# Destination scores split once in bfloat16 parts before the look-up, and 40 key scatters moved behind the first stream's gathers

## The reference

```python
# first graph attention
z  = einsum('ni,hid->nhd', xn, W)
es = einsum('nhd,hd->nh', z, a_src);  ed = einsum('nhd,hd->nh', z, a_dst)
e  = es[src] + ed[dst]
e  = where(e >= 0, e, 0.01 * e)
alpha = exp(e - segment_max(e, dst)[dst]) / segment_sum(..., dst)[dst]
out   = segment_sum(alpha[:, :, None] * z[src], dst)
x = x + out + linear_attention(xn)
# second graph attention, over the layernorm of the new x, 4 experts x 4 heads
e  = leaky_relu(a_src[src] + a_dst[dst], 0.2)     # edges of L0_ffn_edge_index and own edges
...                                                # aggregate, layernorm, top 2 of 4 experts
x = x + sum over experts of gate * (gelu(xn @ W1 + b1) @ W2 + b2)
```

## Time and profile before

| | us |
|---|---|
| median of three runs | 6389.44 |
| lowest and highest run | 6359.07, 6403.71 |
| profiled execution, span from first to last instruction | 6245.5 |
| first look-up stage in it, from POOL's first scatter to DVE's last reduction | 363.4 to 619.8 |
| second look-up stage, from POOL's first gather to DVE's last reduction | 3456.0 to 3632.4 |

### The profile page before, as it was taken

How to read it: one execution, slowest core, us unless ns; L and a number is a source line. 1 busy time by engine, 2 the same in 40 slices (tenths; PEclk the granted TensorE clock), 3 DMA queues, 4 the chain that set the end, 5 groups by cost and what they waited for, 6 DMA issues and landing times. The chain is left out here.

```text
span 6245.5 us, 58318 instructions
## 1 busy us (share of the span) xinstructions
PE 3399.7 (54%) x14771; PEld 2497.0 (40%) x14771; DVE 2946.1 (47%) x6874; ACT 1902.2 (30%) x6108; POOL 3158.9 (51%) x3144
## 2 busy tenths in 40 slices
PE   5554356565666666655552634555455554555660
...
GB/s 109 74 207 166 104 93 95 95 96 91 95 101 106 105 106 109 106 100 96 93 76 52 223 109 24 26 26 27 24 25 31 23 30 24 25 31 22 30 34 248
DMA packets 326836, 508.54 MB, mean 81 GB/s; under 512 B 102092, under 2 KB 249219, under 8 KB 314654
## 3 DMA queue, kind: packets, MB, share of 16 engines
...
...
## 5 line engine op out<-in xcount | busy, mean ns | idle before, releaser
L1440 POOL DMA_INDIRECT gnn_gathered<-gnn_rows,gnn_src x1612 | 1603.5, 995 | 970.2 <-issue 454.4
L1929 POOL DMA_INDIRECT ffn_gathered<-ffn_rows,ffn_src x1216 | 1201.9, 988 | 1249.8 <-DVE ffn_scaled L2335 807.9
L1528 PE MATMUL gnn_step_ps<-gnn_scaled,gnn_dst_onehot 128*128 128x260 f32 x3224 | 1209.8, 517 | 820.2 <-DVE gnn_scaled L1622 585.3
L1467 ACT ACTIVATE gnn_scaled<-gnn_gathered,gnn_edge_weights 128x65 f32<-128x65 f32 x4464 | 1137.4, 336 | 778.2 <-remote 377.5
L1528 PEld LDWEIGHTS gnn_step_ps<-gnn_scaled,gnn_dst_onehot 128*128 128x128 f32 x3224 | 746.7, 252 | 1122.6 <-DVE gnn_scaled L1622 674.2
L1642 DVE TENSOR_TENSOR gnn_sums<-gnn_sums,gnn_step_ps 128x260 f32 x1612 | 680.5, 422 | 623.9 <-PE gnn_step_ps L1528 252.0
L2054 PE MATMUL exp_hidden_ps<-exp_xn_turned,exp_w 128*128 128x512 f32 (+1 forms) x832 | 532.5, 777 | 486.4 <-ACT exp_hidden L2085 342.5
L2238 PE MATMUL ffn_sum_ps<-ffn_scaled,ffn_dst_onehot 128*128 128x24 f32 x2432 | 392.6, 320 | 350.6 <-issue 234.3
L2085 ACT ACTIVATE exp_hidden<-exp_hidden_ps,exp_b 128x512 f32<-128x512 f32 (+1 forms) x208 | 137.8, 663 | 1304.9 <-remote 750.5
L2238 PEld LDWEIGHTS ffn_sum_ps<-ffn_scaled,ffn_dst_onehot 128*128 128x128 f32 x2432 | 392.0, 254 | 356.5 <-issue 235.1
L2054 PEld LDWEIGHTS exp_hidden_ps<-exp_xn_turned,exp_w 128*128 128x128 f32 x832 | 189.8, 253 | 659.0 <-ACT exp_hidden L2085 365.6
...
## 6 DMA issues: line engine op xcount, KB each, us to landing
...
gnn_gathered<-gnn_rows,gnn_src POOLq DMA_INDIRECT x1612
...
```

The lines of the kernel that those rows point to most:

```text
L1440: pool.indirect_dma_start(out=G[:, n, u, :], out_offset=None, in_=d[t + "_rows"], in_offset=bass.IndirectOffsetOnAxis(ap=e.src[:, st:st + ...
L1467: last = act.activation(ZW[:, st % BUF, h * F:(h + 1) * F], G[:, i % 2, u, h * F:(h + 1) * F], ACT.Copy, scale=W[:, i % 2, h, u:u + 1])
L1528: pe.matmul(ps[:, st % BUF, 0:g.row], OH[:, st // PIECE % 2, u % PIECE, :], ZW[:, st % BUF, :], start=True, stop=True).then_inc(multiplied, 1)
L1929: pool.indirect_dma_start(out=self.out[:, j % GATHERED, u, :], out_offset=None, in_=self.rows, in_offset=bass.IndirectOffsetOnAxis(ap=self ...
```

## The change

It has two parts. First, the score rows `ED` (128 partitions x 4 x 128) are split in three bfloat16 parts `EP` once, ahead of the groups, by four DVE operations. `window_hot` becomes bfloat16. `spread_out` picks all three parts, by twelve bfloat16 matmuls of 32 columns instead of four float32 ones. A new loop of ACT, `take`, copies the 128x384 result from PSUM to `LM`. DVE's `divide` goes. This holds for both look-up stages. Second, of the 152 scatters in the first look-up stage the last 40 move to the end of POOL's list in `stream`, behind the 1612 gathers, with a wait until all have landed; SP copies their keys and places into two SBUF tensors of their own in `keep_late`.

```diff
@@ -37,9 +37,10 @@
 LOT = 8
 BIG = 1.0e38
 EPS = 1e-5
-FIRST_UNITS = 192
+FIRST_UNITS = 152
+STREAM_UNITS = 40
 PLACED_WITH_TABLES = 40
-LATE_UNITS = UNITS - FIRST_UNITS
+LATE_UNITS = UNITS - FIRST_UNITS - STREAM_UNITS
 BUNDLE = 26
 BUNDLES = 62
 ROWS = H * (BUNDLE + 1)
@@ -192,20 +193,22 @@
         kept = ctx.enter_context(ExitStack())
         key_max = kept.enter_context(nc.sbuf_tensor("in_k_max", [P, D], F32))
         tables = StepTables(nc, kept, gnn)
+        behind = (kept.enter_context(nc.sbuf_tensor("edges_sorted_behind", [P, STREAM_UNITS * UNIT], F32)),
+                  kept.enter_context(nc.sbuf_tensor("edges_unit_place_behind", [P, STREAM_UNITS], I32)))
         with stage(nc) as sem:
             constants(nc, c, sem)
         with ExitStack() as shared:
-            window_hot = shared.enter_context(nc.sbuf_tensor("gnn_window_onehot", [P, gnn.grid], F32))
+            window_hot = shared.enter_context(nc.sbuf_tensor("gnn_window_onehot", [P, gnn.grid], BF16))
             rows = SortedRows(nc, shared)
             with stage(nc) as sem:
                 nodes_and_keys(nc, c, sem, d, x, gw, gas, gad, wqkv, src, dst, edges, rows, window_ends, key_max, gnn, ffn)
-            scatter = UnitScatter(c, d, rows)
+            scatter = UnitScatter(c, d, rows, behind)
             with stage(nc) as sem:
                 step_tables(nc, c, sem, d, gnn, tables, window_hot, scatter.share)
             with stage(nc) as sem:
                 edge_dst_scores(nc, c, sem, d, gnn, tables, window_hot, scatter.beside_look_up, scatter.keep_late)
         with stage(nc) as sem:
-            acc = stream(nc, kept, c, sem, d, gnn, tables, x, wqkv, wout, gamma, key_max)
+            acc = stream(nc, kept, c, sem, d, gnn, tables, x, wqkv, wout, gamma, key_max, scatter)
             nodes_between(nc, c, sem, d, acc, wgat, fas, fad, scatter)
         kept.close()
         gate = ctx.enter_context(nc.sbuf_tensor("gate_of_expert", [P, TILES, 4], F32))
@@ -213,7 +216,7 @@
             tables = ChunkTables(nc, kept, ffn)
             gather = EdgeGather(nc, kept, c, d, ffn, tables)
             with ExitStack() as shared:
-                window_hot = shared.enter_context(nc.sbuf_tensor("ffn_window_onehot", [P, ffn.grid], F32))
+                window_hot = shared.enter_context(nc.sbuf_tensor("ffn_window_onehot", [P, ffn.grid], BF16))
                 with stage(nc) as sem:
                     chunk_tables(nc, c, sem, d, ffn, tables, window_ends, window_hot)
                 with stage(nc) as sem:
@@ -739,6 +742,7 @@
         wrow_i = sb("_window_rows_i", [B, P], I32)
         before = sb("_end_before", [1, 1])
         WE = sb("_windows_everywhere_i", [P, g.grid], I32)
+        WF = sb("_windows_everywhere", [P, g.grid])
         SE = sb("_step_end_cols", [P, 2 * B])
         SER = sb("_step_end_rows", [2 * B, P])
         BE = sb("_bundle_ends", [NB, 3, S])
@@ -806,8 +810,8 @@
             link(dve.tensor_copy(wrow_i[:], ps[0:B, 0, 0:P]))
             at["line"] = link.n
             dve.wait_ge(line_in, 32)
-            link(dve.tensor_copy(window_hot[:], WE[:]))
-            link(dve.tensor_scalar(window_hot[:], window_hot[:], c.lo[:, 0:1], None, ALU.is_equal))
+            link(dve.tensor_copy(WF[:], WE[:]))
+            link(dve.tensor_scalar(window_hot[:], WF[:], c.lo[:, 0:1], None, ALU.is_equal))
 
             dve.wait_ge(fetched, 16 * B + fetched_before)
             link(dve.tensor_copy(SE[:, 0:B], SR[:, :, 0, 1]))
@@ -916,9 +920,10 @@
     groups = g.grid // S
     assert groups * S == g.grid and groups % 2 == 0
     rows_in = [sem("%s_local_rows_in%d" % (t, n)) for n in range(2)]
-    cleared, turned, kept, spread, taken, chain, split, onehot, looked, scored, apart, sp_apart = (sem(t + "_ed_" + n) for n in (
-        "cleared", "turned", "kept", "spread", "taken", "split_step", "split", "onehot", "looked_up", "scored", "wait_apart",
-        "sp_wait_apart"))
+    cleared, turned, kept, spread, chain, divided, split, onehot, looked, scored, apart, sp_apart, act_apart = (
+        sem(t + "_ed_" + n) for n in (
+            "cleared", "turned", "kept", "spread", "split_step", "divided", "split", "onehot", "looked_up", "scored", "wait_apart",
+            "sp_wait_apart", "act_wait_apart"))
     with ExitStack() as s:
         def sb(name, shape, dt=F32):
             return s.enter_context(nc.sbuf_tensor(t + name, shape, dt))
@@ -926,7 +931,7 @@
         DR = sb("_local_rows_everywhere", [P, 2, S, P], BF16)
         OHT = sb("_dst_onehot_turned", [P, 2, S, P], BF16)
         ED = sb("_dst_score_rows", [P, H, P])
-        T4 = sb("_dst_scores", [P, S, H])
+        EP = sb("_dst_score_parts", [P, 3, H, P], BF16)
         LM = sb("_dst_scores_split", [P, 2, S, 3, H], BF16)
         pd = s.enter_context(nc.psum_tensor(t + "_ed_ps", [P, 2, 512], F32))
         pk = s.enter_context(nc.psum_tensor(t + "_ed_lookup_ps", [P, 2, 512], F32))
@@ -966,22 +971,11 @@
         def _(dve):
             link = Chain(dve, chain)
             dve.memset(ED[:], 0.0).then_inc(cleared, 1)
-
-            def divide(i, n):
-
-                link.n = i * 4
-                if not static(i, 1):
-                    dve.wait_ge(split, i)
-                dve.wait_ge(spread, i + 1)
-                dve.tensor_copy(T4[:], pd[:, 0, 0:H * S].rearrange("p (h u) -> p u h", h=H)).then_inc(taken, 1)
-                if not static(i, 2):
-                    dve.wait_ge(looked, i - 1)
-                dve.wait_ge(taken, i + 1)
-                link(dve.tensor_copy(LM[:, n, :, 0, :], T4[:]))
-                link(dve.tensor_tensor(T4[:], T4[:], LM[:, n, :, 0, :], ALU.subtract))
-                link(dve.tensor_copy(LM[:, n, :, 1, :], T4[:]))
-                link(dve.tensor_tensor(T4[:], T4[:], LM[:, n, :, 1, :], ALU.subtract))
-                dve.tensor_copy(LM[:, n, :, 2, :], T4[:]).then_inc(split, 1)
+            dve.wait_ge(kept, 1)
+            link(dve.tensor_copy(EP[:, 0], ED[:]))
+            link(dve.tensor_tensor(ED[:], ED[:], EP[:, 0], ALU.subtract))
+            link(dve.tensor_copy(EP[:, 1], ED[:]))
+            dve.tensor_tensor(EP[:, 2], ED[:], EP[:, 1], ALU.subtract).then_inc(divided, 1)
 
             def mask(i, n):
                 dve.wait_ge(rows_in[n], x_count(i, n) + 16)
@@ -997,16 +991,12 @@
                                   pk[:, n, 0:S * 3 * H].rearrange("p (u q h) -> p u h q", q=3, h=H), AX.X, ALU.add
                                   ).then_inc(scored, 1)
 
-            divide(0, 0)
             mask(0, 0)
-            divide(1, 1)
             mask(1, 1)
             collect(0, 0)
             with dve.Fori(1, groups // 2) as j:
-                divide(j * 2, 0)
                 mask(j * 2, 0)
                 collect(j * 2 - 1, 1)
-                divide(j * 2 + 1, 1)
                 mask(j * 2 + 1, 1)
                 collect(j * 2, 0)
             collect(groups - 1, 1)
@@ -1015,11 +1005,13 @@
         @block.tensor
         def _(pe):
             def spread_out(i, n):
-                if not static(i, 1):
-                    pe.wait_ge(taken, i)
-                for h in range(H):
-                    last = pe.matmul(pd[:, 0, h * S:(h + 1) * S], ED[:, h, :], window_hot[:, bass.ds(i * S, S)],
-                                     start=True, stop=True)
+                if not static(i, 2):
+                    pe.wait_ge(split, i - 1)
+                for q in range(3):
+                    for h in range(H):
+                        k = (q * H + h) * S
+                        last = pe.matmul(pd[:, n, k:k + S], EP[:, q, h, :], window_hot[:, bass.ds(i * S, S)],
+                                         start=True, stop=True)
                 last.then_inc(spread, 1)
 
             def look_up(i, n):
@@ -1035,7 +1027,7 @@
             for h in range(H):
                 last = pe.transpose(pd[0:2 * HIS, 1, h * P:(h + 1) * P], score[:, 1, :, h], c.ident[:])
             last.then_inc(turned, 1)
-            pe.wait_ge(kept, 1)
+            pe.wait_ge(divided, 1)
             spread_out(0, 0)
             spread_out(1, 1)
             look_up(0, 0)
@@ -1051,6 +1043,15 @@
             act.wait_ge(cleared, 1)
             act.wait_ge(turned, 1)
             act.copy(ED[0:2 * HIS, :, :], pd[0:2 * HIS, 1, :].rearrange("p (h i) -> p h i", h=H)).then_inc(kept, 1)
+
+            def take(i, n):
+                if not static(i, 2):
+                    act.wait_ge(looked, i - 1)
+                    stand_apart(act, act_apart)
+                act.wait_ge(spread, i + 1)
+                act.copy(LM[:, n], pd[:, n, 0:3 * H * S].rearrange("p (q h u) -> p u q h", q=3, h=H)).then_inc(split, 1)
+
+            pairs(act, take)
 
 
 class Mix:
@@ -1320,7 +1321,7 @@
             dve.bn_aggr(self.MV[:], self.ST[:]).then_inc(self.measured, 1)
 
 
-def stream(nc, kept, c, sem, d, g, e, x, wqkv, wout, gamma, key_max):
+def stream(nc, kept, c, sem, d, g, e, x, wqkv, wout, gamma, key_max, scatter):
 
 
     t = g.tag
@@ -1440,6 +1441,7 @@
```

(23 more changed lines are left out.)

## The result

| | before, us | after, us |
|---|---|---|
| median of six runs | 6371.04 | 6414.07 |
| lowest and highest | 6352.21, 6403.71 | 6407.06, 6431.05 |
| profiled execution, span | 6245.5 | 6411.0 (its own time 6412.83) |

The ratio is 1.0065 with the interval 1.0040 to 1.0091. The forecast was 6342 us, 47 less, and the range ended at 6380: wrong in sign and outside the range, though still within the 1% called no change.

What follows compares the result with a forecast made beforehand. No engine was taken to bound the whole, so stages were read by their last engine. Without crawls the first look-up stage gains 48 us, the second 0, the stream costs 1: 6389.4 - 47 = 6342 us, range 6305 to 6380.

Steps and rivals of the forecast that it cites:

- the sum: Whole kernel, no crawl before or after: first stage gains 48 us, second 0, stream costs 1, together 47 us.
- crawl: Look-up stages: PE's instructions come one at a time, 0.5 to 2 us of "issue" between them, cause unknown.
- The two slow stretches: Profile before: DVE lost 52 us in the first look-up stage and 15 us in the second.
- First stage: First look-up stage: end moves from 594 to 546 us without a crawl, 48 us gained.
- The prices: Look-up groups: picks 0.6 us, ACT's copy 0.52 us, loads 3.35 us in the first stage, 3.1 in the second.
- POOL beside the masks: First look-up stage: each mask adds 0.709 us to POOL, which ends at 542.7; at 506 if only bandwidth were shared.
- the prediction's two terms: POOL in the first look-up stage: 1.272 us a scatter with its pause, plus 0.709 us for each mask.
- Behind the stream: End of the first stream: 40 scatters take 50.9 us of POOL's 57 us idle, 2 for landing; 1 us lost.
- Second stage: Second look-up stage: POOL sets the end at 3625; 7 us gained against the profiled crawl, 0 without one.
- Rival C: Look-up stages: denser PE matmuls lengthen the crawl, first stage ends at 650, 6446 us in all; chance 0.06.
- Its counterargument: Against Rival C: in the first look-up stage PE issued at the same rate from 364 to 520 without any crawl.
- Rivals A and B: Whole kernel: A, crawl before and gone after, 6309 us, chance 0.24; B, crawl in both, 6364 us, chance 0.20.

Runs made afterwards that it cites:

- before_third: The kernel before, unchanged, profiled on chip 8, a slow chip: 6380.17 us.
- before_again: The kernel before, unchanged, profiled on chip 13, a fast chip: 0.9989 of before's 4986.71 us.
- after_fourth: The kernel after, unchanged, profiled on chip 8, a slow chip: 6415.01 us.
- slow_pe_after: The kernel after with three PE semaphore increments behind each look-up-stage matmul but a group's last, chip 8: 7833.77 us, 1.2265 of before.
- slow_pe_before: The kernel before with three PE semaphore increments behind each look-up-stage matmul but a group's last, chip 8: 7445.75 us, 1.1657 of before.
- after_again: The kernel after, unchanged, profiled on chip 13, a fast chip: 4934.43 us, 0.9898 of before.
- free_pool: The kernel after with 72 scatters instead of 112 beside the first look-up and 40 more in `nodes_between`: 4973.06 us, 0.9973 of before.
- ahead_72: The kernel after with 72 gathers instead of 112 beside the second look-up, chip 5: 4942.38 us, 0.9929 of before.
- slow_pe: The pair slow_pe_before and slow_pe_after, PE slowed by semaphore increments in the look-up stages: 7445.75 and 7833.77 us.
- split_only_2: The kernel before with the split and bfloat16 picks but no scatters moved, chip 3: 6393.31 us, 1.0035 of before.
- dense_pe: The kernel after with each look-up matmul issued twice, 76 PE matmuls a group instead of 44: 0.9904 of before's 4984.36 us.
- sparse_pe: The kernel after with 16 look-up matmuls of 24 columns instead of 32 of 12, another output: 0.9892 of before's 4984.36 us.

## Why the prediction was wrong

*The step that failed* is the one in the sum that took the timed executions to have no crawl, "before or after", because the profiled one was short. The same kernel before takes 4977 to 4987 us on chips without it. In before_third PE's waits under "issue" are 350 us in the edges and 220 in the stream, where before_again has none; so much of the 1390 us between the two is crawl for certain, and for the rest the runs don't say how it comes about. The two slow stretches of the earlier trace rows were the part of it that stood out. The sign of the edits turns with it, by the differences of before_third and after_fourth: first stage -39, stream +17, tail +40, `nodes_between` and the tables after it +16, second stage +22, edges -13, the rest -8, in all +35. The stream's +17 and the +16 have no change of code behind them, and I leave them as scatter between executions: from the first scatter of `nodes_between` to the second stage before_third has 233 us and after_fourth 249, but slow_pe_after 229 and slow_pe_before, with before's code there, 254. Of the 35 us only -39, +40 and +22 are tied to the edits, 23 in all.

*First stage.* -48 forecast; -50 without the crawl (242 to 192), -39 with. DVE's own end followed the loads, at 3.5 us a group rather than 3.35, and POOL's last scatter came at 540 where 542.7 was forecast. The move made 41 of the 50 us by itself, the split 5. With the crawl the gain comes in another way: 40 scatters fewer end POOL's issuing earlier, and the rest of the groups runs at 3.3 us.

*The prices.* Twelve picks took 0.49 us (25.3 / 52) where 0.6 was taken, and 0.63 with the crawl (33.0 / 52); ACT's copy took 479 ns (0.52). The loads came next, as forecast: DVE waits 91.1 us for them in after_again, by its groups by line:

```profile
L984 DVE TENSOR_SCALAR gnn_dst_onehot_turned<-nn_local_rows_everywhere,iota_lo 128x4096 bf16<-128x4096 bf16 x52 | 67.9, 1306 | 91.1 <-DMA nn_local_rows_everywhere<-gnn_local_rows 91.1
L1013 PE MATMUL gnn_ed_ps<-gnn_window_onehot,gnn_dst_score_parts 128*128 (+1 forms) x624 | 25.3, 188 | 3.1 <-DVE gnn_dst_score_parts L978 3.1
L1052 ACT CAST gnn_dst_scores_split<-gnn_ed_ps 128x384 bf16<-128x384 f32 x52 | 24.8, 479 | 154.2 <-PE gnn_ed_ps L1013 132.8 <-PE gnn_ed_lookup_ps L1023 18.5 <-issue 3.0
```

*POOL beside the masks.* POOL's end came within 3 us of the sum with the masks 10% closer together, so each mask still stopped POOL for about 0.7 us. With nothing for the masks POOL would have ended at 506. A better test is the same 112 scatters beside 31 masks in after and beside 50 in after_again:

```profile
L1741 POOL DMA_INDIRECT ffn_keys<-edges_sorted,edges_unit_place x112 | 129.4, 1155 | 56.0 <-issue 32.3 <-POOLq L152 14.2 <-PE gnn_ed_lookup_ps L1023 8.6
```
```profile
L1741 POOL DMA_INDIRECT ffn_keys<-edges_sorted,edges_unit_place x112 | 143.0, 1277 | 48.3 <-issue 32.0 <-POOLq L152 14.5 <-PE gnn_ed_lookup_ps L1023 0.9
```

(143.0 - 129.4) / 19 = 0.72 us a mask, and free_pool's 72 scatters beside 32 masks took 92.8 us where the prediction's two terms give 92.9. This agrees with the exclusive lock that the Trainium skill describes in "SBUF — State Buffer", section "SBUF: two separate sides"; that it is the lock, and not another cause that goes with each mask, isn't shown.

*Behind the stream.* 1 us forecast, bounds 0 to 5. Without the crawl it is 9 (59 to 68), since landing and the end of the block take 9.2 us, not 2, and POOL's list ended 1.4 us behind DVE's: a mis-sized term. With it 40: there the term is of another kind. The step looked for idle time on POOL's list and took PE's and DVE's as fixed; but the tail is PE's and DVE's work, and beside POOL's issuing it got slower.

*Second stage.* 0 to -7 forecast. Without the crawl -5, POOL setting the end (ahead_72). With it +22 to +27: twelve bfloat16 picks in place of four float32 ones cost nothing on a PE that has time. That they cost there because 44 matmuls take the place of 36 is argued, not shown. For it: slow_pe, and the second stage's period, 4.7 to 6.1 us. Against it: the first stage's period beside POOL's scatters didn't grow with the same eight matmuls (5.4 us in before_third, 5.1 in after_fourth and in split_only_2). `dense_pe` or `sparse_pe` with the crawl would tell, and had no such run.

*Rival C*, with 0.06, came nearest: more matmuls meet a crawl. It had no part for POOL, and it looked to the first stage, where ending POOL's list early outweighs any loss, and not to the second, where all 112 gathers stay. Its counterargument ("the same rate from 364 to 520 without any") was read off the one exceptional execution. It is a fact all the same: 100 scatters and 40 masks went by there without a crawl, on a program that crawls beside POOL in every other trace of its kind, and the runs don't say why. Rivals A and B had the crawl as something that happens or doesn't, of fixed length.

*What stays open*: why the chips differ (chip 13 was without a crawl both times it came, the others came once, so the time or the machine around the chip isn't ruled out), and what in POOL's indirect DMAs holds the other engines' instructions back on some. The runs show where it happens and what ends it, not the path (semaphores, memory, the way instructions reach the engines). Transfers of code don't show it: the pages of before_again and before_third both have 100 and 181 packets on the two instruction queues, at 0.1% of the DMA engines' time each. A kernel in which POOL's issuing is spread so that no stage of many small matmuls has it beside was not tried.
